# Decoder layer on one core: self attention scores by four row tiles, formed a second time transposed with the maximum subtracted in PSUM

## The chip, the core and the metric

One core of a Trainium2 chip runs the whole layer in one launch. The metric is the device time in microseconds (us); the kernel before took 193.94 us, the median of 3 runs (193.43 to 194.21). All positions in time below count from the first instruction of the profiled execution.

## What is computed

x has 16 sequences of 64 tokens and 128 features; all arithmetic is float32.

```python
x = x + self_attn(layernorm(x))          # 16 heads of 8, rotary embedding, softmax over 64 keys
x = x + cross_attn(layernorm(x), ctx)    # 8 heads of 64, context 16 x 64 x 96
x = x + moe(layernorm(x))                # 2 shared experts + top 2 of 8 experts, SwiGLU, F = 176
# self attention, per sequence b and head h:
attn = softmax(einsum('bhsd,bhtd->bhst', rope(q) * 8**-0.5, rope(k)))
out  = einsum('bhst,bhtd->bhsd', attn, v)
```

## The kernel before

The kernel is one hand ordered program for each engine; each engine works its own list from top to bottom, and semaphores tie the lists together. The chain of TensorE calls is at the end of the tensor block (lines 1185 to 1275), that of ScalarE at 530 to 608, of VectorE at 820 to 916 and of GpSimd at 356 to 398.

**Self attention (units 0 to 15).** Sequences go in four quads of 4 sequences (256 tokens); heads in four groups g of 4 heads. A unit u is quad u // 4, group u % 4. `queries_keys(quad)` projects (L930 to L932, lines of a helper of three float16 matmuls), `rotate(quad)` on VectorE adds bias and rotates (L660, L672). The heads are told apart by masks: `mask_q` writes q four times, once per group with the other rows zero, into qG (L316 on GpSimd; the first quad by `mask_q0`, L679 on VectorE), and `mask_k` writes k four times, once per head of a group, into kM (L323; first quad L452 on ScalarE, second L686 on VectorE). `scores(u)` is then 4 matmuls with all 128 rows (L1006: 64 weight columns, 256 moving columns, two column tiles). Each float32 matmul shows as two records. `shift(u)` on VectorE takes the maximum (L695) and subtracts it on the way out of PSUM (L698), `exponentials(u)` on ScalarE writes ex (L460), `transpose_p(u)` transposes it by 4 matmuls with the identity (L1037), `copy_t(u)` brings that to PT (L469). After four units `attend(quad)` multiplies with the values (L1058) and with ones (L1064, the sums); `divide_ot` divides (L712, L716), `bias_ot` adds the bias (L494), `project_o(hf)` projects half of the tokens (L1076), `add_x2(hf)` adds x. Scores use banks 0 to 2 in turn, so up to three units are under way.

**Cross attention (units 16 to 23)** follows in the same pattern, with `copy_xq`, `shift`, `sums`, `divide` (GpSimd, L346), `transpose_p`, `copy_t`, `cross_attend`, `cross_project`. It needs x2 of the half: `statistics` (L624, L627), `inverse_std` on GpSimd (L308, L310), `normalise` (L638), `transpose_xn` (L959), `copy_xnT` (L430), `rest_xnT` (L647). **The experts** come last (`expert_up`, `spread_w`, `expert_down`; lines 1130 to 1181).

**What else sets the order.** Banks 6 and 7 are handed round by the list MISC: projection i of that list waits until entry i - 2 has been read out, by ScalarE (`copy_v` L445, `copy_cv` L487, `copy_xq` L500, `copy_kx` L414) or VectorE. The expert weights come in 14 chunks through two staging buffers: SP issues the DMA of chunk c when c - 1 chunks are finished (L285, L289), ScalarE casts each chunk to float16 (`chunk_float16`, L425), GpSimd forms the rest (`split_chunk`, L332) and by that frees the buffer. A ScalarE cast waits in its list until the chunk has landed. `MISC` reads, ahead of the experts:

```python
MISC = (["ln1_0", "k_0", "q_0", "k_1", "q_1", "ln1_1", "v_0", "cv_0", "cv_1", "k_2", "q_2", "v_1",
         "k_3", "q_3", "cv_2", "cv_3", "wo_0", "ln2_0", "kx_4"] ...
```

Of the kernel before, what the change touches and what calls it, by code (L numbers as in the profile page):

```python
# [55 lines left out]
         "k_3", "q_3", "cv_2", "cv_3", "wo_0", "ln2_0", "kx_4"]  # L56
# [7 lines left out]
def decoder_layer(nc, x, ctxT, attn_w, attn_b, bias_rows, xw_q, xw_k, xw_v, xw_o, gate_w, w_gate, w_up,  # L64
# [4 lines left out]
    with ctx:  # L69
# [33 lines left out]
        consts_sb = sb("consts_sb", [P, D + HG + 2 + G + E * E + 2 * 32])  # L103
# [12 lines left out]
        OT = t12  # L116
# [46 lines left out]
        sbank = lambda u: bank[u % 3]  # L163
        tbank = lambda u: bank[3 + u % 2]
# [27 lines left out]
        q0_masked = sem("q0_masked")  # L192
        q_masked = sem("q_masked")
        k_masked = sem("k_masked")
        s_full = sem("s_full")
# [55 lines left out]
        CHUNK_AT = [3, 4, 7, 8, 10, 11, 12, 13, 16, 17, 18, 20, 21]  # L251
        assert len(CHUNK_AT) == len(CHUNKS) + 1
# [44 lines left out]
        def _(pool):  # L297
# [15 lines left out]
            def mask_q(quad):  # L313

                pool.wait_ge(q_rotated, quad + 1)
                nc.gpsimd.tensor_tensor(qG[:, :, quad * QT:(quad + 1) * QT],  # L316
                                        qr[:, quad % 2, :].unsqueeze(1).broadcast_to([D, G, QT]),
                                        mask_g.unsqueeze(2).broadcast_to([D, G, QT]), ALU.mult).then_inc(q_masked, 1)

            def mask_k(quad):  # L320

                pool.wait_ge(k_rotated, quad + 1)
                nc.gpsimd.tensor_tensor(  # L323
                    kM[:, 4 * quad:4 * quad + 4],
                    kr[:, quad % 2, :].rearrange("p (b t) -> p b t", t=S).unsqueeze(2).broadcast_to([D, 4, HG, S]),
                    mask_h4.unsqueeze(1).unsqueeze(3).broadcast_to([D, 4, HG, S]), ALU.mult).then_inc(k_masked, 1)
# [15 lines left out]
            def divide(u):  # L342

                pool.wait_ge(r_ready, u - NU1 + 1)
                v = ex[:, u % NE, :].rearrange("p (c t) -> p c t", t=S)
                nc.gpsimd.tensor_tensor(v, v, rs[:, u % NE, :].unsqueeze(2).broadcast_to([P, BLK, S]),  # L346
                                        ALU.mult).then_inc(p_ready, 1)
# [14 lines left out]
            rest([xwq_sb[:, i] for i in range(2)], xwq_raw, 2)  # L362
            nc.gpsimd.memset(VM[:], 0.0).then_inc(zeroed, 1)
            nc.gpsimd.memset(wT[:], 0.0).then_inc(zeroed, 1)
# [4 lines left out]
            nc.gpsimd.memset(PTx[:], 0.0).then_inc(zeroed, 1)  # L369
            mask_q(1)  # L370
            mask_q(2)
            mask_k(2)
            for c in range(3):
                split_chunk(c)
            mask_q(3)
            mask_k(3)
            for c in range(3, 8):
                split_chunk(c)
            inverse_std(2)
            split_chunk(8)  # L380
            x2_bias(0)
            for u in range(NU1, NU):
                divide(u)
                if u == 16:
                    inverse_std(3)
                if u == 17:
                    split_chunk(9)
                    split_chunk(10)
                if u == 19:
                    x2_bias(1)  # L390
                if u == 23:
                    inverse_std(4)
                if u in (20, 21):
                    split_chunk(u - 9)
# [6 lines left out]
        def _(act):  # L401
# [30 lines left out]
            def copy_v(hf):  # L432

                if hf == 0:
                    act.wait_ge(zeroed, 1)
# [19 lines left out]

            def exponentials(u):
                act.wait_ge(s_sub, u + 1)
                if u >= NE:
                    act.wait_ge(t_full, u - NE + 1)
                nc.scalar.activation(ex[:, u % NE, :], sh[:, u % 2, :], ACT.Exp,  # L460
                                     scale=SCALE1 if u < NU1 else SCALE2).then_inc(e_ready, 1)

            def copy_t(u):

                act.wait_ge(t_full, u + 1)
                if u < NU1:
                    if u >= NPT:
                        act.wait_ge(pv_full, (u - NPT) // 4 + 1)
                    nc.scalar.copy(PT[:, u % NPT, :], tbank(u)[:, :]).then_inc(t_copied, 1)  # L469
                else:  # L470
                    if u == NU1:
                        act.wait_ge(zeroed, 3)
                    if u >= NU1 + 2:
                        act.wait_ge(pv_full, 4 + u - 2 - NU1 + 1)
                    src = tbank(u)[:, :].rearrange("p (c s) -> p c s", s=S)
                    for j in range(2):
                        r = slice(j * S, (j + 1) * S)
                        ins = nc.scalar.copy(PTx[r, u % 2, :, j, :], src[r])  # L478
                    ins.then_inc(t_copied, 1)
# [16 lines left out]
            def copy_xq(hf):  # L496
                act.wait_ge(s_full, NU1 if hf else NU1 // 2)
# [42 lines left out]
            for j in range(NU + 4):  # L540
                if j == 16:
                    copy_t(14)
                    copy_t(15)
                if j == 18:
                    copy_kx(7)
                    copy_t(16)
                    copy_xnT(2, 1)
                    copy_cv(4)
                if j == 19:
                    copy_xq(1)  # L550
                    copy_t(17)
                    copy_otx(0)
                if j == 15:
                    copy_kx(4)
                if j == 17:
                    bias_ot(3)
                if j < NU:
                    exponentials(j)
                if j == 0:
                    copy_xnT(1, 1)  # L560
                    copy_v(0)
                if j in (1, 2):
                    copy_cv(j - 1)
                if j in (9, 12):
                    bias_ot(j // 3 - 3)
                if j == 16:
                    bias_ot(2)
                if 2 <= j < NU + 2 and not 16 <= j <= 19:
                    copy_t(j - 2)
                if j == 3:  # L570
                    copy_kx(3)
                if j == 4:
                    copy_v(1)
                if j in (9, 12):
                    copy_cv(j // 3 - 1)
                if j == 14:
                    copy_xnT(2, 0)
                if j == 15:
                    copy_xq(0)
                if j == 16:  # L580
                    copy_kx(5)
                if j == 17:
                    copy_kx(6)
                if NU1 < j - 3 < NU:
                    copy_otx(j - 3 - NU1)
                if j == 25:
# [748 lines left out]
```

## Time and profile before

| | |
|---|---|
| runs, median (lowest to highest) | 193.94 us (193.43 to 194.21) |
| profiled execution, span from first to last instruction | 190.1 us |
| its own device time | not listed beside the runs; the median lies 3.8 us above the span |
| TensorE matmuls busy | 165.1 us, 87% |
| TensorE weight loads busy | 103.2 us, 54% |
| VectorE, ScalarE, GpSimd busy | 134.7, 115.7, 81.8 us |
| mean granted clock of TensorE | 0.986 |

Busy time of TensorE counts overlapping matmuls once, and ends are modelled, so how long a group of matmuls holds the engine is read from the start of one group to the start of the next. The chain that ended last spends 53% of the span on TensorE, 16% on VectorE, 14% on ScalarE, 5% on GpSimd. Lines such as L930 to L932 belong to a helper and carry the projections of all stages.

### The profile page before, as it was taken

How to read it: one execution, taken by the hardware profiler on the slowest of the kernel's cores; microseconds unless marked ns; L12 is line 12 of the kernel's file. 1: busy time of each engine (PE TensorE's matmuls, PEld its weight loads, DVE VectorE, ACT ScalarE, POOL GpSimd, SP SyncE). 2: the span in 40 equal slices, each digit the busy share in tenths (PEclk: the TensorE clock that was granted, in tenths of full speed). 3: DMA queues.
4: the chain of work that ended last, by engine and by line, in shares of the span. 5: the costliest groups of instructions: out<-in, count | busy, mean ns of one | idle time of the engine just before them, and what ended most of it. 6: DMA issues, size and time to landing. Idle time of an engine off the chain costs nothing.

```text
span 190.1 us, 4163 instructions
## 1 busy us (share of the span) xinstructions
PE 165.1 (87%) x1599; PEld 103.2 (54%) x1599; DVE 134.7 (71%) x279; ACT 115.7 (61%) x227; POOL 81.8 (43%) x78
## 2 busy tenths in 40 slices
PE   7576985999999689849999799997998799999992
PEld 2134543665657346635757687653664566666661
DVE  3468998969989627986184554888787987556642
ACT  2148178795788385658779974653649344555450
POOL 1459560847445000763052440074443455544540
PEclk9999999999999999996999999999999999999997
DMA  5980000031221200100000000000000001000001
GB/s 143 304 280 0 0 2 3 0 84 56 59 58 57 78 0 3 59 14 2 10 0 3 2 3 0 0 5 0 0 3 2 0 3 38 17 0 3 2 3 55
DMA packets 6900, 6.43 MB, mean 34 GB/s; under 512 B 736, under 2 KB 5312, under 8 KB 6880
## 3 DMA queue, kind: packets, MB, share of 16 engines
q1 hardware_dynamic: 6480, 5.63, 10.0%
q10 hardware_dynamic: 400, 0.53, 0.9%
q8 instruction: 13, 0.21, 0.5%
q14 instruction: 7, 0.06, 0.1%
HBM read 5.63 MB, written 0.52 MB: 32 GB/s over the span
## 4 chain that ended last, share of the span: by engine, by line
PE 53%; DVE 16%; ACT 14%; issue 7%; POOL 5%; DMA 3%; POOLq 1%; DVEq 0%; ACTq 0%
PE bank L930 6%; PE bank L1006 6%; PE bank L932 6%; PE bank L931 6%; DVE xn_sb L638 4%; PE bank L1175 4%; PE bank L1037 4%; PE bank L1100 4%; ACT Vx L487 3%; PE bank L1110 3%; DMA x_sb<-x_dram 3%; PE bank L1179 2%; POOL rstd L310 2%; PE bank L1159 2%; ACT ex L460 2%
## 5 line engine op out<-in xcount | busy, mean ns | idle before, releaser
L339 POOL TENSOR_TENSOR qG<-qG 128x512 f16<-128x512 f32 (+1 forms) x26 | 30.1, 1157 | 38.4 <-ACT qG L527 38.3
L520 ACT ACTIVATE qG<-bank 128x512 f32<-128x512 f32 (+1 forms) x28 | 16.7, 597 | 24.4 <-PE bank L932 24.4
L798 DVE TENSOR_TENSOR qG<-bank,qG 128x512 f32<-128x512 f32 (+1 forms) x28 | 19.3, 690 | 13.0 <-PE bank L932 11.5
L695 DVE TENSOR_REDUCE mx<-bank 128x8 f32<-128x512 f32 x24 | 16.3, 680 | 6.1 <-PE bank L1022 4.5
L527 ACT CAST qG<-qG 128x512 f16<-128x512 f32 (+1 forms) x28 | 17.1, 612 | 5.5 <-DVE qG L802 3.5
L460 ACT ACTIVATE ex<-sh 128x512 f32<-128x512 f32 x24 | 15.2, 632 | 6.6 <-DVE sh L698 6.5
L1006 PE MATMUL bank<-kM,qG 128*64 128x256 f32 x128 | 16.9, 390 | 1.3 <-DVE qG L679 1.3
L1175 PEld LDWEIGHTS bank<-wd_sb,qG 128*128 128x128 f16 (+1 forms) x224 | 14.7, 98 | 6.2 <-ACT qG L527 0.7
L698 DVE TENSOR_TENSOR sh<-bank,mx 128x512 f32<-128x512 f32 x24 | 16.6, 692 | 1.6 <-ACT ex L460 0.8
L1175 PE MATMUL bank<-wd_sb,qG 128*128 128x128 f16 (+1 forms) x224 | 17.1, 219 | 0.6 <-ACT qG L527 0.6
L802 DVE TENSOR_TENSOR qG<-bank,qG 128x512 f32<-128x512 f32 x22 | 15.2, 692 | 0.7
L1037 PE MATMUL bank<-consts_sb,ex 128*128 128x128 f32 x96 | 14.8, 277 | 0.0
L1037 PEld LDWEIGHTS bank<-consts_sb,ex 128*128 128x128 f32 x96 | 11.1, 141 | 6.3 <-issue 5.3
L332 POOL TENSOR_TENSOR wd_sb<-stage,wd_sb 128x512 f16<-128x512 f32 (+2 forms) x5 | 4.3, 864 | 20.7 <-ACT wd_sb L425 20.7
L487 ACT COPY Vx<-bank 64x256 f32<-64x256 f32 x32 | 11.7, 367 | 2.3 <-PE bank L990 1.9
L346 POOL TENSOR_TENSOR ex<-ex,rs 128x512 f32<-128x512 f32 x8 | 8.4, 1044 | 11.0 <-DVE rs L707 11.0
L469 ACT COPY PT<-bank 128x512 f32<-128x512 f32 x16 | 9.3, 586 | 3.9 <-PE bank L1037 3.8
L950 PE MATMUL bank<-ctxT_sb,xwk_sb 128*128 128x512 f32 x16 | 10.4, 738 | 1.3 <-issue 1.3
L1006 PEld LDWEIGHTS bank<-kM,qG 128*64 128x64 f32 x128 | 8.0, 136 | 6.4 <-issue 2.2
L1100 PE MATMUL bank<-PTx,Vx 128*64 128x128 f32 x128 | 9.6, 296 | 2.0 <-ACT PTx L478 2.0
L414 ACT ACTIVATE kxM<-bank,consts_sb 128x512 f32<-128x512 f32 x16 | 10.0, 684 | 1.7 <-PE bank L950 1.7
L1179 PE MATMUL bank<-wd_sb,qG 128*128 128x128 f16 (+1 forms) x112 | 10.8, 219 | 0.1
(131 smaller groups left out, 380.7 us busy)
## 6 DMA issues: line engine op xcount, KB each, us to landing
stage<-w_gate_dram SPq DMA_DIRECT2D x3, 256.0 KB, 6.6
stage<-w_up_dram SPq DMA_DIRECT2D x3, 256.0 KB, 2.6
stage<-w_down_dram SPq DMA_DIRECT2D x3, 256.0 KB, 2.9
x_sb<-x_dram SPq DMA_DIRECT2D x2, 256.0 KB, 5.7
out_dram<-x_sb SPq DMA_DIRECT2D x2, 256.0 KB, 2.3
ctxT_sb<-ctxT_dram ACTq DMA_DIRECT2D x1, 384.0 KB, 4.7
sel_sb<-selector_dram SPq DMA_DIRECT2D x1, 352.0 KB, 6.4
qG<-attn_w_dram SPq DMA_DIRECT2D x1, 320.0 KB, 5.9
```

The costliest lines, as they stand in the source:

```text
L339: nc.gpsimd.tensor_tensor(hs[0:r, u % 2, 1, :], hh[0:r, u % 2, :], hs[0:r, u % 2, 0, :], ALU.subtract).then_inc(h_lo, 1)
L460: nc.scalar.activation(ex[:, u % NE, :], sh[:, u % 2, :], ACT.Exp, scale=SCALE1 if u < NU1 else SCALE2).then_inc(e_ready, 1)
L487: ins = nc.scalar.copy(Vx[h2 * S:(h2 + 1) * S, 2 * p + b2, :, :], src)
L520: nc.scalar.activation(sg[0:r, u % 2, :], gbank(u)[0:r, :], ACT.Silu).then_inc(sg_ready, 1)
L527: nc.scalar.copy(hs[0:r, u % 2, 0, :], hh[0:r, u % 2, :]).then_inc(h_hi, 1)
L695: link(nc.vector.reduce_max(mx[:, u % 2, :], v, AX.X))
L698: nc.vector.tensor_tensor(sh[:, u % 2, :].rearrange("p (c t) -> p c t", t=S), v, mx[:, u % 2, :].unsqueeze(2).broadcast_to([P, BLK, S]), A ...
L798: nc.vector.tensor_tensor(dst, ubank(u)[0:r, :], sg[0:r, u % 2, :], ALU.mult).then_inc(hu_ready, 1)
L1006: ins = mm(sbank(u)[b2 * S:(b2 + 1) * S, pp * HG * S:(pp + 1) * HG * S], qG[:, g, b * S:(b + 1) * S], kM[:, b].rearrange("p i t -> p (i t) ...
L1037: ins = nc.tensor.transpose(tbank(u)[:, c * P:(c + 1) * P], ex[:, u % NE, c * P:(c + 1) * P], ident)
L1100: ins = mm(o[c * S:(c + 1) * S, j, :, b2, :], Vx[:, 2 * p + b2, hp, :], PTx[:, u % 2, 2 * hp + b2, :, :], start=True, stop=True)
L1175: mm(pvb[:, n * P:(n + 1) * P], hs[0:r, u % 2, 0, n * P:(n + 1) * P], w[s], start=(first and n == 0 and s == 0), stop=False, skip_group_ch ...
```

## The change

The scores of self attention are formed twice per quad. qG, `mask_q`, `mask_q0`, `mask_k1` and the self attention calls of `shift`, `transpose_p` and `copy_t` go. `first_scores(quad)` works on the rotated q itself in four row tiles of 32 rows (one per group of heads) and two column tiles, into banks 0 to 3. `maxima` reduces each bank to 128x8 into ms. `transpose_max` turns the maxima by 4 matmuls into bank 4, `copy_mT` copies them to mT. `shifted_scores` then overwrites banks 0 to 3: one matmul per row tile, with two rows, writes minus the maximum into all 512 columns, and 8 matmuls per row tile (k as weights, 128 columns; q moving, 64 columns) add the scores transposed. `exponentials` reads that from PSUM and writes PT. `NPT` is 8; PTx of cross attention now lies in PT, OT has memory of its own, ms lies in sh and mT in ex.

```diff
+            def first_scores(quad):
+                pe.wait_ge(q_rotated, quad + 1)
+                pe.wait_ge(k_masked, quad + 1)
+                if quad == 0:
+                    pe.wait_ge(kx_free, 1)
+                else:
+                    pe.wait_ge(e_ready, 4 * quad)
+                for pp in range(2):
+                    for b2 in range(2):
+                        b = 4 * quad + 2 * pp + b2
+                        for g in range(G):
+                            r = slice(32 * g, 32 * (g + 1))
+                            t = (2 * pp + b2) * S
+                            ins = mm(qbank(g)[b2 * S:(b2 + 1) * S, pp * HG * S:(pp + 1) * HG * S],
+                                     qr[r, quad % 2, t:t + S], kM[r, b].rearrange("p i t -> p (i t)"),
...
+            def transpose_max(quad):
+                pe.wait_ge(max_ready, 4 * quad + 4)
...
+                for c in range(HG):
+                    ins = nc.tensor.transpose(mbank[:, c * P:(c + 1) * P], ms[:, c, :], ident)
+            def shifted_scores(quad):
+                pe.wait_ge(mT_copied, quad + 1)
+                for g in range(G):
+                    r = slice(32 * g, 32 * g + 2)
+                    mm(qbank(g)[:, :], minus_h[r, :], mT[r, :], start=True, stop=False, skip_group_check=True)
+                for c in range(HG):
+                    pp, a = c // 2, c % 2
+                    for b2 in range(2):
+                        b = 4 * quad + 2 * pp + b2
+                        for g in range(G):
...
+                            ins = mm(qbank(g)[:, (2 * c + b2) * S:(2 * c + b2 + 1) * S],
+                                     kM[r, b, 2 * a:2 * a + 2].rearrange("p i t -> p (i t)"),
+                                     qr[r, quad % 2, t:t + S], start=False, stop=last, skip_group_check=True)
```

The new orders, condensed, each in its engine's list (p counts the cross units from 0; several calls stand on one line):

```
TensorE
    first_scores(0)
    context_keys(3)
    transpose_xn(1, 1)
    values(0)
    transpose_max(0)
    context_values(0)
    shifted_scores(0)
    first_scores(1)
    context_values(1)
    queries_keys(2)
    attend(0)
    transpose_max(1)
    values(1)
    shifted_scores(1)
    context_values(2)
    first_scores(2)
    queries_keys(3)
    attend(1)
    transpose_max(2)
    context_values(3)
    shifted_scores(2)
    project_o(0)
    first_scores(3)
    attend(2)
    context_keys(4)
    transpose_max(3)
    shifted_scores(3)
    transpose_xn(2, 0)
    cross_queries(0)
    context_keys(5)
    attend(3)
    cross_scores(0)
    cross_scores(1)
    context_keys(6)
    project_o(1)
    cross_scores(2)
    cross_scores(3)
    context_keys(7)
    transpose_p(0)
    context_values(4)
    transpose_xn(2, 1)
...
VectorE
    rotate(0)
    normalise(1, x_sb)
    rotate(1)
    for quad in range(4):
        for g in range(G):
            maxima(4 * quad + g)
        if quad == 0: rest_xnT(1), rotate(2)
        if quad == 1: divide_ot(0), rotate(3), the split of gate_sb
        if quad == 2: divide_ot(1), add_x2(0), statistics(2)
        if quad == 3: normalise(2), divide_ot(2), rest_xnT(2)
    divide_ot(3), shift(0), shift(1), sums(0), add_x2(1), statistics(3), sums(1), normalise(3)
...
ScalarE
    copy_kx(3), copy_xnT(1, 1)
    for quad in range(4):
        copy_mT(quad)
        for g in range(G):
            exponentials(4 * quad + g)
        if quad == 0: copy_v(0), copy_cv(0), copy_cv(1), chunk_float16(0)
        if quad == 1: copy_v(1), bias_ot(0), copy_cv(2), chunk_float16(1), chunk_float16(2)
        if quad == 2: bias_ot(1), copy_cv(3), chunk_float16(3), (4), (5)
    copy_kx(4), copy_xnT(2, 0), bias_ot(2), copy_xq(0), copy_kx(5), copy_kx(6), bias_ot(3)
    chunk_float16(6), (7), cross_exponentials(0), chunk_float16(8), cross_exponentials(1), chunk_float16(9)
...
GpSimd
    memset(ms); memset(VM); mask_k(1); memset(wT); xb_sb; mask_k(2); split_chunk(0); mask_k(3)
    split_chunk(1) to split_chunk(5)
    pool.wait_ge(pv_full, 3)
    nc.gpsimd.memset(PT[:, 0:4, :], 0.0)
    inverse_std(2); x2_bias(0); split_chunk(6) to split_chunk(8)
    divide(0); inverse_std(3); divide(1) ...
```

In MISC "cv_2" moves ahead of "k_3" and "kx_4" ahead of "ln2_0".

## Rows read from the trace of the kernel before

**Rows 1.** The page of before: busy time by engine; granted clock of TensorE in 40 slices of 4.75 us.
```profile
PE 165.1 (87%) x1599; PEld 103.2 (54%) x1599; DVE 134.7 (71%) x279; ACT 115.7 (61%) x227; POOL 81.8 (43%) x78
...
PEclk9999999999999999996999999999999999999997
```

**Rows 2.** Windows: length, busy us of PE, PEld, DVE, ACT, POOL (instructions), granted clock, DMA.
```profile
34.00:58.00 24.00, 24.00 (x314) 14.83 (x314) 21.11 (x34) 19.82 (x45) 13.84 (x10) 1.00 0.20 55
...
83.00:86.00 3.00, 1.40 (x12) 1.26 (x14) 2.79 (x6) 0.99 (x3) 0.86 (x1) 0.94 0.08 22
85.00:88.00 3.00, 3.00 (x25) 2.23 (x23) 2.76 (x6) 2.67 (x7) 0.00 (x0) 0.61 0.07 19
...
120.00:190.00 70.00, 62.83 (x551) 38.48 (x548) 49.94 (x91) 35.54 (x61) 31.32 (x28) 0.99 0.03 9
```

**Rows 3.** Timeline of TensorE, 84.6 us: the second half's normalised x2 is transposed.
```profile
84.61 0.63 PE L959 MATMUL bank<-consts_sb,xn_sb 128*128 128x128 f32 x4 [2.40 <-DVE xn_sb L638]
```

**Rows 4.** Timeline of TensorE in self attention: start, length, line, shape, count.
```profile
50.95 1.10 PE L1058 MATMUL bank<-PT,VM 128*32 128x64 f32 x64
51.87 1.05 PE L1064 MATMUL bank<-PT,consts_sb 128*32 128x256 f32 x16
52.84 0.66 PE L1037 MATMUL bank<-consts_sb,ex 128*128 128x128 f32 x4
53.43 1.08 PE L1006 MATMUL bank<-kM,qG 128*64 128x256 f32 x8
54.45 1.12 PE L990 MATMUL bank<-xwv_sb,ctxT_sb 128*128 128x512 f32 x2
55.41 0.60 PE L1037 MATMUL bank<-consts_sb,ex 128*128 128x128 f32 x4
```

**Rows 5.** Groups by line and shape on VectorE and ScalarE.
```profile
L695 DVE TENSOR_REDUCE mx<-bank 128x8 f32<-128x512 f32 x24 | 16.3, 680 | 6.1 <-PE bank L1022 4.5 <-PE bank L1006 1.4
...
L520 ACT ACTIVATE qG<-bank 128x512 f32<-128x512 f32 x26 | 15.5, 597 | 24.2 <-PE bank L932 24.2
...
L712 DVE RECIPROCAL rsum<-bank 128x256 f32<-128x256 f32 x4 | 7.0, 1753 | 0.5 <-PE bank L1064 0.4
```

**Rows 6.** Groups by line and shape, weight loads: busy, mean ns of one | idle before.
```profile
L1006 PEld LDWEIGHTS bank<-kM,qG 128*64 128x64 f32 x128 | 8.0, 136 | 6.4 <-issue 2.2 <-DVE qG L679 1.6
L1110 PEld LDWEIGHTS bank<-xwo_sb,t 128*128 128x128 f32 x64 | 7.7, 191 | 1.7 <-issue 1.5 <-DVE xb_sb L733 0.2
...
L1058 PEld LDWEIGHTS bank<-PT,VM 128*32 128x32 f32 x256 | 3.8, 110 | 1.1 <-issue 0.7 <-ACT PT L469 0.4
```

**Rows 7.** Timeline of ScalarE, 16 us: the key mask of the first quad.
```profile
16.09 1.71 ACT L452 ACTIVATE kM<-qkr,consts_sb 128x256 f32<-128x256 f32 x4 [0.63 <-DVE qkr L672]
```

**Rows 8.** Timeline of all engines, 25 to 32 us: a projection waits for bank copies.
```profile
25.52 1.73 ACT L445 COPY VM<-bank 64x128 f32<-64x128 f32 x8 [1.26 <-PE bank L932]
...
27.93 1.50 ACT L487 COPY Vx<-bank 64x256 f32<-64x256 f32 x4
...
30.52 0.87 DVE L660 SCALAR_TENSOR_TENSOR t<-bank,attn_b_sb,rope_sb 128x256 f32<-128x256 f32 x2
31.43 0.42 DVE L672 TENSOR_TENSOR qkr<-t 128x256 f32<-128x256 f32 x1
...
31.67 0.28 PE L930 MATMUL bank<-xnT,attn_w_sb 128*128 128x256 f16 x1 [1.28 <-ACT Vx L487]
```

**Rows 9.** DMA issues: KB each, median us from issue to landing.
```profile
stage<-w_up_dram SPq DMA_DIRECT2D x3, 256.0 KB, 2.6
stage<-w_down_dram SPq DMA_DIRECT2D x3, 256.0 KB, 2.9
```

**Rows 10.** Groups by line and shape on GpSimd.
```profile
L310 POOL TENSOR_TENSOR rstd<-ve,minus_half 128x4 f32<-128x4 f32 x6 | 6.2, 1039 | 0.5
...
L332 POOL TENSOR_TENSOR wd_sb<-stage,wd_sb 128x512 f16<-128x512 f32 x3 | 3.5, 1155 | 18.8 <-ACT wd_sb L425 18.8
...
L369 POOL MEMSET PTx<- 128x2048 f32 x1 | 1.8, 1796 | 0.0
```

More of the change, by code:

```diff
@@ L454, in mask_k0, with copy_mT @@
                 ins.then_inc(k_masked, 1)
-            def exponentials(u):
[L457 to L479, printed above, removed]
+            def copy_mT(quad):
+                act.wait_ge(mT_full, quad + 1)
+                if quad:
+                    act.wait_ge(shifted_full, 4 * quad)
+                nc.scalar.copy(mT, mbank[:, :]).then_inc(mT_copied, 1)
@@ new lines, in copy_t @@
+            def copy_t(p):
+                act.wait_ge(t_full, p + 1)
+                if p == 0:
+                    act.wait_ge(zeroed, 4)
+                if p >= 2:
+                    act.wait_ge(pv_full, 4 + p - 2 + 1)
+                src = tbank(p)[:, :].rearrange("p (c s) -> p c s", s=S)
+                for j in range(2):
+                    r = slice(j * S, (j + 1) * S)
+                    ins = nc.scalar.copy(PTx[r, p % 2, :, j, :], src[r])
+                ins.then_inc(t_copied, 1)
@@ L539, in _ @@
             copy_kx(2)
[L540 to L560, printed above, removed]
-                    copy_v(0)
[L562 to L572, printed above, removed]
-                    copy_v(1)
[L574 to L586, printed above, removed]
-                    copy_xnT(3, 0)
-                if j == 19:
-                    copy_cv(5)
-                if j == 20:
-                    copy_cv(6)
-                if j == 21:
-                    copy_cv(7)
-                if j == 27:
-                    router_exp(0)
-                if j in CHUNK_AT:
-                    chunk_float16(CHUNK_AT.index(j))
@@ new lines, in _ @@
+            copy_kx(4)
+            copy_xnT(2, 0)
+            bias_ot(2)
+            copy_xq(0)
+            copy_kx(5)
+            copy_kx(6)
+            bias_ot(3)
+            chunk_float16(6)
+            chunk_float16(7)
+            cross_exponentials(0)
+            chunk_float16(8)
+            cross_exponentials(1)
+            chunk_float16(9)
+            copy_kx(7)
+            copy_t(0)
+            copy_xnT(2, 1)
+            copy_cv(4)
+            cross_exponentials(2)
+            chunk_float16(10)
@@ new lines, in _ @@
+            copy_xq(1)
+            copy_t(1)
+            copy_otx(0)
+            cross_exponentials(3)
+            copy_cv(5)
+            for p in range(4, NT + 3):
+                if p < NT:
+                    cross_exponentials(p)
+                if p - 2 < NT:
+                    copy_t(p - 2)
+                copy_otx(p - 3)
+                if p in (4, 5):
+                    copy_cv(p + 2)
+                    chunk_float16(p + 7)
+                if p == NT + 1:
+                    copy_xnT(3, 0)
@@ L1038, in transpose_p @@
                 ins.then_inc(t_full, 1)
             def attend(quad):
[L1043 removed]
+                pe.wait_ge(e_ready, 4 * quad + 4)
                 if quad % 2 == 0:
@@ new lines, in _ @@
+            first_scores(3)
+            attend(2)
+            context_keys(4)
+            transpose_max(3)
+            shifted_scores(3)
+            transpose_xn(2, 0)
+            cross_queries(0)
+            context_keys(5)
+            attend(3)
+            cross_scores(0)
+            cross_scores(1)
+            context_keys(6)
+            project_o(1)
+            cross_scores(2)
+            cross_scores(3)
+            context_keys(7)
+            transpose_p(0)
+            context_values(4)
@@ L1256, in _ @@
+            for p in range(4, NT):
+                transpose_p(p)
+                cross_attend(p - 1)
+                cross_project(p - 2)
             transpose_xn(3, 0)
```

434 lines of the change are left out of this document (205 added, 229 removed).

## The prediction

> **What bounds the kernel now.** I read the page first. TensorE is busy 87% of the span, at the full granted clock but for one slice [rows 1]. The windows say where: from 34 to 58 us, in self attention, TensorE is never idle, while VectorE is busy for 21.1 and ScalarE for 19.8 of the 24 us [rows 2]. This stage is bound by TensorE's list, with two engines close behind, and it is dense because three score banks keep units in different phases. The experts (120 to 190 us) are not touched; what the change does must show in when cross attention can go on. The landmark for that is the transposition of the normalised second half of x2, at 84.61 us, for which TensorE had waited 2.40 us [rows 3]; behind it the two kernels' lists have nearly the same order. So I walk the new lists to that instruction and compare.
>
> **What goes.** Sixteen units of scores at 1.02 us (53.43 to 54.45) and of transposes at 0.59 (52.84 to 53.43) [rows 4]: 25.8 us of TensorE. On VectorE go 16 subtractions and masks, on ScalarE 16 copies, on GpSimd three q masks. None of it is a gain by itself; it must come off the chain.
>
> **What comes, per quad.** First scores: 16 matmuls of 256 columns, 32 records. Before, 8 records in two column tiles took 1.02 us [rows 4]. If the four row tiles run beside each other, 32 records in 8 tiles are again four deep: 1.0 us; if not, 4.1. Four maxima of 0.68 us [rows 5] overlap a little: 2.5 us. The copy of the turned maxima takes 0.6, as L520 does out of PSUM [rows 5]. Four transposes pass 512 columns once, half of what L990 does in 0.96 (54.45 to 55.41), and took 0.59 behind tiled work [rows 4]; I read 0.15 of that as the change of tiling, and count 0.5 for the turn, and 0.15 ahead of each tiled group. Shifted scores: 8 records of 512 columns in four tiles are two deep, as L990's two records: 0.96 us. Then 64 records with 128 weight columns and only 64 moving ones. The attend has 64 records with 32 weight columns in four column tiles: 0.92 us (50.95 to 51.87), 14 ns each [rows 4]. But a load of 32, 64 and 128 columns lasts 110, 136 and 191 ns [rows 6], some 0.84 ns a column, so 128 columns should hold a tile for about 107 ns (an estimate from that slope); 16 deep, that is 1.7 us, 1.9 with gaps. Together 3.0 us. Lower end 1.9, if the loads hide as the attend's do; upper end 8, if loads of different row tiles queue (64 x 0.107 = 6.8 in place of 1.9), and 10.8 if the 512-column matmuls queue too. I take 3.0: the attend's 14 ns lie below the 27 that a 32-column load needs by the slope, so tiles do load beside each other. Four exponentials out of PSUM, 0.60 each [rows 5], take 2.15 in a row.
>
> A rule of the Trainium skill speaks against this part: TensorE: Matmul & The Clock Gate, section LDWEIGHTS, has a 32x128 load take as long as a 128x128 one, since only columns count. The columns' part agrees (110, 136, 191 ns [rows 6]); no row here shows a 32-row load. With the rule the shifted scores take 3.0 us, and if fewer rows did load faster, 1.9, which is some 3 us less over the quads. The same page, section on packing small matmuls, measured 3.07x for four row tiles of 512 columns; by that the four-fold steps take 1.3 us where I have 1.0, and the sum would be about 1 us more.
>
> **The waits.** Banks 0 to 3 hold both passes, so the first scores of a quad wait for all four exponentials of the quad before: quads no longer overlap. Walk, with 0.05 to 0.15 us from engine to engine:
>
> Quad 0. First scores start at 17.85, behind the key mask that ends at 17.80 [rows 7]. VectorE now does normalise and rotate(1) ahead of the maxima, so these run from 22.0 to 24.5. Turned 25.0; context_values(0) to 26.1 (its bank is freed by rest_xnT(1), behind the maxima); shifted scores to 29.1; exponentials to 31.4.
>
> Quad 1. The maxima stand behind rotate(2) on VectorE, rotate(2) needs queries_keys(2), and that needs banks 7 and 6 read out by copy_cv(0) and copy_cv(1), which now stand behind all four exponentials and copy_v(0): 31.4 + 1.73 + 1.5 + 1.5 = 36.15. Before, the same wait ended at 31.67 [rows 8]. Then q's projection 0.7, rotation 0.87 + 0.42 [rows 8], maxima to 40.8, turned and copied 42.0, shifted scores to 45.05, exponentials 47.35.
>
> Quad 2. copy_v(1), bias 0.5 and copy_cv(2) end at 51.1; projection, rotation and the gate's split at 53.5; maxima 56.0; shifted 60.3; exponentials 62.6. The period is some 15.5 us; before, TensorE's own work set it, 4 x 1.6 + 1.9 for the attend (50.95 to 52.84) [rows 4] = 8.3, and the projections in between.
>
> Quad 3. project_o(0) stands ahead of first scores and waits for bias_ot(1), behind the exponentials: first scores end at 65.25. add_x2 and statistics stand ahead of the maxima: 66.4 to 68.9. copy_mT(3) stands behind the cast of chunk 5, whose DMA waits for split_chunk(3) (66.4) and lands 2.6 later [rows 9]: copied 70.3, shifted 73.35, exponentials 75.65.
>
> First half of x2. GpSimd does split_chunk(5) (70.9), the clear of 2048 columns, 1.80 us, and only then inverse_std(2), 1.04 and a little [rows 10]: 74.0. Normalise 75.7; divide_ot(2), 1.75 [rows 5] + 0.43, stands ahead of rest_xnT(2): 78.6. cross_queries(0), context_keys(5), attend(3): 84.3.
>
> Second half. divide_ot(3) to 86.65; bias_ot(3) stands behind copy_kx(6): 88.95; project_o(1) 90.1; sums(0), ahead of add_x2(1), needs an exponential that stands behind chunks 6 and 7: statistics end at 93.35. Chunk 8's DMA can start only after split_chunk(6) (90.8) and lands 2.9 later [rows 9], cast 94.3. GpSimd does split_chunk(8) 1.16, divide(0) 1.04, inverse_std(3) 1.3 [rows 10]: 97.8; normalise, with GpSimd at work beside it, 2.4: 100.3.
>
> **Sum.** 100.3 - 84.6 = 15.7 us later. The granted clock adds to it: before, it read 0.94 around that wait of 2.40 us and 0.61 in the 3 us from 85 [rows 2, 3]. In the new lists TensorE waits like that, for 1 to 3 us at a time, in each quad, so shifted scores or attends will partly run at 1.2 GHz in place of 2.4. Half of an attend and of a shifted score (2.5 us) is lost per quad where it strikes; I put 2 us on it in all, from 0 to 7. 190.1 + 17.7 = 207.8 us of span; the runs' median lies 3.8 above the span: 211.6, and I say 211.
>
> The Trainium skill, TensorE: Matmul & The Clock Gate, section Loop structure matters more than you think, warns that long waits between bursts of matmuls let the clock drop; by that rule each quad would lose its 2.5 us, and the time would be about 216. The 0.61 agrees with it, and the full clock in 34 to 58 us shows the dense case.
>
> **Rivals.** (a) Row tiles do not run beside each other, or their loads queue: the change does not do what it says. Shifted scores take 8 to 10.8 us instead of 3.0, in three quads wholly on the path: 15 to 23 more, and first scores 2 more: 226 to 236. For: no row shows row tiles. Against: column tiles overlap, loads included. (b) Much of the delay is absorbed: shifted scores take 1.9 (3.3 less), the clock stays up (2 less), and the late bias_ot(3) and chunk 8 (2.3 + 3.5) hide: 211.6 - 11.1 = 200.5, 197 to 203. Against: the path to the landmark goes through both. (c) Faster: TensorE stays the bound. 25.8 us go, 4 x (1.0 + 0.6 + 3.0) = 18.4 come: 7.4 less, 186.5. Its place is the wait for banks 7 and 6 ahead of rotate(2) and rotate(3); it decides if those cost nothing and other work fills the quad's own chain, 1.0 + 2.5 + 0.5 + 0.6 + 3.0 + 2.15 and 0.7 of hand-overs = 10.5 us. Against: 10.5 is itself above 8.3, and one set of banks forbids filling it.
>
> **Chances.** My walk 0.73, (a) 0.12, (b) 0.09, (c) 0.04, no change 0.02. A measurement of this kernel can tell 0.5% from none. The walk's own bounds: 2 of clock, 3.3 of loads and 2 of hand-overs down; 5 of clock and 4 of waits up: 204 to 220. The range, 201 to 222, takes in a part of (b) and leaves (a) and (c) out.
>
> **What would show it.** First scores of a quad right behind the last exponential of the quad before; VectorE idle for some 9 us ahead of quad 1's maxima; 14 to 17 us per quad; the first exponential of quad 1 at about 45, of quad 3 at about 73; the landmark at 99 to 104; a clock below 1 in slices between 35 and 65 us; the experts 70 us as before. Wrong if the period is under 10 us, if the shifted scores take over 5, or if the landmark comes before 90.

## The result: 224.8 us, 16% slower, and the profile after

The kernel with the two passes takes 224.83 us, the median of 4 runs (222.39 to 226.20); the kernel before, run beside it, 193.69 us. The ratio is 1.159, with a 95% interval of 1.150 to 1.168. The forecast was 211, from 201 to 222: the sign was right, the size was not. The profiled execution is the slowest of the four (226.2 us, span 224.4), so positions read from it can lie a microsecond or two later than in the median run.

The page of after, to be read against [rows 1]: busy time by engine, and the granted clock in slices of 5.6 us.

```profile
PE 180.4 (80%) x1839; PEld 113.8 (51%) x1839; DVE 125.9 (56%) x255; ACT 108.8 (48%) x215; POOL 78.6 (35%) x77
...
PEclk9999655875875569569955999999999999999997
```

TensorE is busy for 15 us more, though it was to have 7 less to do, and through self attention its clock is never full for long. The windows of after, with the columns of [rows 2], give the amounts:

```profile
17.00:35.00 18.00, 12.54 (x134) 7.93 (x132) 8.65 (x16) 5.91 (x12) 6.67 (x4) 0.70 0.00 1
35.00:55.00 20.00, 16.02 (x216) 10.16 (x216) 8.00 (x12) 7.19 (x22) 3.18 (x2) 0.67 0.06 16
55.00:75.00 20.00, 14.19 (x204) 8.56 (x202) 9.87 (x14) 6.24 (x19) 4.29 (x3) 0.67 0.07 20
75.00:90.00 15.00, 10.70 (x206) 7.22 (x202) 6.56 (x18) 6.93 (x16) 7.09 (x7) 0.73 0.16 45
90.00:105.00 15.00, 12.26 (x132) 6.30 (x132) 5.73 (x7) 6.87 (x14) 0.00 (x0) 0.70 0.00 1
...
155.00:224.00 69.00, 62.09 (x547) 38.27 (x545) 49.30 (x90) 34.83 (x61) 31.30 (x28) 0.99 0.03 9
```

VectorE and ScalarE, once close behind TensorE [rows 2], are busy for 8.00 and 7.19 of 20 us. The experts take their 70 us as before. Nearly all the loss lies ahead of the landmark, which came 33.7 us later, at 118.31 and not 84.61 [rows 3]; the span grew by 34.3. TensorE's timeline in after (L1001 first scores, L1015 turn of the maxima, L1023 minus the maximum, L1032 scores transposed, L1107 project_o, L954 the landmark):

```profile
17.88 1.12 PE L1001 MATMUL bank<-kM,qkr 32*64 32x256 f32 x32 [0.17 <-issue]
...
25.18 1.11 PE L1015 MATMUL bank<-consts_sb,sh 128*128 128x128 f32 x4 [2.94 <-DVE sh L690]
...
27.93 2.09 PE L1023 MATMUL bank<-ex,consts_sb 2*128 2x512 f32 x8
29.80 3.53 PE L1032 MATMUL bank<-qkr,kM 32*128 32x64 f32 x64
35.56 2.01 PE L1001 MATMUL bank<-kM,qkr 32*64 32x256 f32 x32 [2.23 <-ACT PT L467]
...
41.17 0.28 PE L925 MATMUL bank<-xnT,attn_w_sb 128*128 128x256 f16 x1 [0.32 <-ACT Vx L495]
...
47.00 0.66 PE L1015 MATMUL bank<-consts_sb,sh 128*128 128x128 f32 x4 [3.11 <-DVE sh L690]
...
77.96 2.05 PE L1107 MATMUL bank<-wo_sb,OT 128*128 128x128 f32 x8 [2.57 <-issue]
...
86.07 1.14 PE L1023 MATMUL bank<-ex,consts_sb 2*128 2x512 f32 x8 [0.68 <-ACT ex L460]
87.03 1.91 PE L1032 MATMUL bank<-qkr,kM 32*128 32x64 f32 x64
...
118.31 1.09 PE L954 MATMUL bank<-consts_sb,xn_sb 128*128 128x128 f32 x4 [1.30 <-DVE xn_sb L646]
```

The same instructions stand here at both clocks. Quad 3's shifted scores take 0.96 us to 87.03 and 1.9 more; quad 0's take 1.87 to 29.80 and then 3.53. Ahead of quad 0's, TensorE had waited 2.94 us for the maxima. From 25.2 to 36 us the granted clock reads 0.50 throughout. The turned maxima of quads 0 to 3 begin at 25.18, 47.00, 67.24 and 84.79: 21.8, 20.2 and 17.6 us apart, about 20 in the mean. VectorE in after (L668 and L680 rotation, L690 maxima, L842 split of the gate):

```profile
21.30 1.43 DVE L680 TENSOR_TENSOR qkr<-t 128x256 f32<-128x256 f32 x1
22.66 2.47 DVE L690 TENSOR_REDUCE sh<-bank 128x8 f32<-128x512 f32 x4
...
40.96 0.88 DVE L668 SCALAR_TENSOR_TENSOR t<-bank,attn_b_sb,rope_sb 128x256 f32<-128x256 f32 x2 [15.24 <-PE bank L927]
...
59.06 0.88 DVE L668 SCALAR_TENSOR_TENSOR t<-bank,attn_b_sb,rope_sb 128x256 f32<-128x256 f32 x2 [10.00 <-PE bank L927]
...
62.57 1.12 DVE L842 CAST gate_sb<-gate_raw 128x8 f16<-128x8 f32 x1
```

The waits of 15.24 and 10.00 us stand where the forecast had its wait for banks 6 and 7, but the banks are only a part of them. Behind quad 0's exponentials TensorE has first scores and context values to do, at half clock (35.56 to 39.4); the projection of quad 2's k then starts at once, and that of q waits 0.32 us for a bank copy (41.17). New against the forecast are the addition of 1.43 us, 0.42 in [rows 8], and 1.12 us for a cast of 8 columns.

### The profile page after: what moved, and what is told of

It reads as the page before. It is cut to its first block, busy times and chain, and to the rows that moved or that the text cites. A ratio compares the mean times of both kernels' runs of the same rounds, so it can differ in the third digit from the quotient of the medians.

```text
span 224.4 us, 4553 instructions
## 1 busy us (share of the span) xinstructions
PE 180.4 (80%) x1839; PEld 113.8 (51%) x1839; DVE 125.9 (56%) x255; ACT 108.8 (48%) x215; POOL 78.6 (35%) x77
## 4 chain that ended last, share of the span: by engine, by line
PE 54%; ACT 14%; DVE 13%; issue 10%; POOL 5%; DMA 2%; POOLq 1%; DVEq 0%; ACTq 0%
PE bank L925 6%; PE bank L926 5%; PE bank L927 5%; PE bank L1032 5%; PE bank L1205 3%; DVE sh L690 3%; PE bank L1023 3%; PE bank L1130 3%; PE bank L985 3%; PE bank L945 3%; DVE xn_sb L646 3%; PE bank L1140 2%; ACT PT L467 2%; DMA x_sb<-x_dram 2%; PE bank L1001 2%
## 5 line engine op out<-in xcount | busy, mean ns | idle before, releaser
L798 DVE TENSOR_TENSOR qG<-bank,qG 128x512 f32<-128x512 f32 (+1 forms) x28 | 19.3, 690 | 12.9 <-PE bank L927 11.5
L668 DVE SCALAR_TENSOR_TENSOR t<-bank,attn_b_sb,rope_sb 128x256 f32<-128x256 f32 x16 | 7.0, 476 | 26.6 <-PE bank L927 26.6
L467 ACT ACTIVATE PT<-bank 128x512 f32<-128x512 f32 x16 | 8.3, 602 | 21.4 <-PE bank L1032 21.4
L1205 PE MATMUL bank<-wd_sb,qG 128*128 128x128 f16 (+1 forms) x224 | 17.1, 219 | 0.6 <-ACT qG L534 0.6
L322 POOL TENSOR_TENSOR kM<-qkr,consts_sb 128x1024 f32<-128x1024 f32 x3 | 5.7, 1892 | 33.6 <-DVE qkr L680 33.6
L1032 PEld LDWEIGHTS bank<-qkr,kM 32*128 32x128 f32 x256 | 13.1, 293 | 3.5 <-issue 3.5
L985 PE MATMUL bank<-xwv_sb,ctxT_sb 128*128 128x512 f32 x16 | 13.1, 912 | 0.0
L646 DVE TENSOR_SCALAR xn_sb<-x_sb,mv,rstd 128x128 f32<-128x128 f32 x16 | 8.9, 683 | 6.9 <-POOL rstd L315 6.9
L1032 PE MATMUL bank<-qkr,kM 32*128 32x64 f32 x256 | 12.5, 374 | 0.0
L1015 PE MATMUL bank<-consts_sb,sh 128*128 128x128 f32 x16 | 3.5, 357 | 10.9 <-DVE sh L690 10.9
L715 DVE RECIPROCAL rsum<-bank 128x256 f32<-128x256 f32 x4 | 7.0, 1746 | 8.4 <-PE bank L1095 8.4
L1130 PE MATMUL bank<-PT,Vx 128*64 128x128 f32 x128 | 9.6, 296 | 2.0 <-ACT PT L486 2.0
```

Of the source, the lines that this page charges most:

```text
L646: ins = nc.vector.tensor_scalar(xn_sb[:, hf, n, :], src[:, hf * TPH + n, :], mv[:, hf, n, 0:1], rstd[:, hf, n:n + 1], ALU.subtract, ALU.mult)
L798: nc.vector.tensor_tensor(dst, ubank(u)[0:r, :], sg[0:r, u % 2, :], ALU.mult).then_inc(hu_ready, 1)
L985: mm(ps[:, :], ctxT_sb[:, p * P:(p + 1) * P], xwv_sb[:, :], start=True, stop=True).then_inc(full, 1)
L1032: ins = mm(qbank(g)[:, (2 * c + b2) * S:(2 * c + b2 + 1) * S], kM[r, b, 2 * a:2 * a + 2].rearrange("p i t -> p (i t)"), qr[r, quad % 2, t: ...
L1130: ins = mm(o[c * S:(c + 1) * S, j, :, b2, :], Vx[:, 2 * p + b2, hp, :], PTx[:, p % 2, 2 * hp + b2, :, :], start=True, stop=True)
L1205: mm(pvb[:, n * P:(n + 1) * P], hs[0:r, u % 2, 0, n * P:(n + 1) * P], w[s], start=(first and n == 0 and s == 0), stop=False, skip_group_ch ...
```

## The experiments

Theories after this reading. **Clock**: half the speed in self attention makes up what the forecast lacks. **Order**: the lists, not the added work, make the period; the projections of the next quads, and the copies that free banks 6 and 7 for them, sit behind work that doesn't need them. **Contention**: VectorE is held by GpSimd. **Second pass**: the added work itself is what costs. The medians in this part stand beside runs of the kernel before, which lie between 192.1 and 193.7 by chip. Not all kernels ran on one chip, so the difference of two kernels is given by medians and, in brackets, by ratios times 193.5 us.

**e1_fill.** The lists as in after; in the long waits TensorE multiplies something nobody reads.

```diff
+            def fill(n, copied): ...
+                for _ in range(n):
+                    mm(mbank[:, :], sel_sb[:, 0:P], sel_sb[:, 512:1024], start=True, stop=True)
+            fill(12, 0)    # ahead of transpose_max(0); seven more groups of 3 to 18
```

> The changed kernel with idle matmuls put ahead of the waits of TensorE in self attention (into bank 4, 80 of 128x512 float16 in eight places), lists otherwise as they are. Theory clock: 13 us of the 31 lost are work at 1.2 GHz on the path; with the waits filled the granted clock of 17 to 110 us goes from 0.7 to over 0.95 and the time from 224.8 to about 211 to 214. Rival order: the clock is low only where TensorE waits anyway, the path is set by ScalarE's and VectorE's lists: under 3 us gained, 222 or more.

Measured: 214.3 us, ratio 1.111 (1.102 to 1.120), 0.3 us above the clock theory's range. TensorE's timeline in e1_fill, and its windows from 17 to 90 us:

```profile
25.16 0.66 PE L1015 MATMUL bank<-consts_sb,sh 128*128 128x128 f32 x4 [0.35 <-DVE sh L690]
...
27.77 1.91 PE L1032 MATMUL bank<-qkr,kM 32*128 32x64 f32 x64
...
41.99 0.66 PE L1015 MATMUL bank<-consts_sb,sh 128*128 128x128 f32 x4
...
79.78 4.00 PE L1079 MATMUL bank<-sel_sb 128*128 128x512 f16 x9
...
105.95 1.08 PE L954 MATMUL bank<-consts_sb,xn_sb 128*128 128x128 f32 x4 [1.31 <-DVE xn_sb L646]
```
```profile
17.00:35.00 18.00, 16.20 (x194) 8.73 (x192) 8.60 (x18) 10.02 (x27) 6.65 (x4) 1.00 0.00 1
35.00:55.00 20.00, 16.45 (x320) 10.38 (x321) 11.24 (x19) 9.32 (x25) 5.81 (x4) 1.00 0.06 16
55.00:75.00 20.00, 18.49 (x275) 10.55 (x276) 10.58 (x21) 6.48 (x14) 5.95 (x6) 1.00 0.19 50
75.00:90.00 15.00, 12.14 (x155) 6.14 (x153) 5.14 (x8) 7.91 (x14) 2.82 (x4) 0.77 0.02 5
```

Quad 0's maxima are ready at the same 25.2 us; from there the full clock saves 5.0 us by quad 1 (47.00 to 41.99), 8.1 by quad 2, 12.9 by quad 3 (84.79 to 71.89). The clock costs at least 224.8 - 214.3 = 10.5 us (9.3 by the ratios); at least, since behind 75 us it still read 0.77. There the idle matmuls themselves got in the way: nine of them took 4.00 us from 79.78, at half clock, and cross_queries(0) began behind them at 83.62, though its last input had been written by 81.61.

**e2_order.** The work of after, in another order. ScalarE: copy_v, copy_cv and bias_ot(1) go ahead of each quad's exponentials. TensorE: queries_keys(2) and (3) ahead of the next first scores. VectorE: rest_xnT(1) ahead of the maxima.

```diff
 ScalarE, in quad 0
             copy_mT(quad)
+            copy_v(0); copy_cv(0); copy_cv(1)
             exponentials(...)
-            copy_v(0); copy_cv(0); copy_cv(1)
```

> The changed kernel with the copies of values and context values (copy_v, copy_cv, bias_ot(1)) moved on ScalarE ahead of the exponentials of their quad, their matmuls and queries_keys(2) and (3) ahead of first_scores of the next quad, rest_xnT(1) ahead of the maxima. Nothing added or left out. Theory order: the 15 us and 10 us in which VectorE waited for the projections of quads 1 and 2 go, a quad takes 10.5 to 12 us in place of 18 to 21, and since TensorE waits less the clock comes back too: 197 to 204 us. Rival clock alone: TensorE still waits for maxima and exponentials in each quad, the clock stays at half, and less than 10 us are gained: 215 or more.

Measured: 205.08 us, ratio 1.067 (1.055 to 1.078), 1 us above the theory's range and far from the rival's. The turned maxima now begin at 25.95, 38.23, 51.64 and 62.10. With no idle matmul much of the clock is back too: 0.91 in 17 to 35 us, 1.00 in 35 to 55, then 0.80 in 55 to 75. So the order is worth 19.8 us (17.8), a part of which is clock. How the 19.8 divide, and which of the moves on the three engines gave most, was not tested.

**e4_fill_order.** e2 with 25 idle matmuls in the waits that remain.

> The new order of e2_order with idle matmuls in five of its waits (25 in all, 16 of them in the second half of x2's path). If the order alone brings the clock back, within 2 us of e2_order; if in e2_order the clock stays low in self attention, 3 to 8 us less than e2_order.

Measured: 206.56 us, ratio 1.062 (1.048 to 1.077), not to be told from e2. The clock of 17 to 55 us is 1.00 in e4, and quad 3's turned maxima begin at 61.37 and not 62.10: in self attention the clock had 0.7 us more to give.

**e3_mask.** After, with one wait more: mask_k on GpSimd waits until q is rotated too, so that it no longer runs beside the addition.

```diff
                 pool.wait_ge(k_rotated, quad + 1)
+                pool.wait_ge(q_rotated, quad + 1)
```

> The changed kernel with GpSimd's mask_k(quad) waiting for the rotated q as well as the rotated k. Theory contention: the addition that rotates q (1.43 us in place of 0.42 beside mask_k) is back at 0.42 in three quads, two of them on the path, one with the split of the gate weights behind it: 2 to 4 us gained, 221 to 223. Rival: the mask comes as much later as the addition gains, or the addition is slow for another reason: within 1 us of 224.8.

Measured: 215.23 us, ratio 1.114 (1.103 to 1.125), 9.6 us (8.7) less than after, where 2 to 4 were expected. VectorE, GpSimd and TensorE in e3_mask:

```profile
21.68 0.42 DVE L681 TENSOR_TENSOR qkr<-t 128x256 f32<-128x256 f32 x1
```
```profile
22.24 1.89 POOL L323 TENSOR_TENSOR kM<-qkr,consts_sb 128x1024 f32<-128x1024 f32 x1 [3.28 <-DVE qkr L681]
```
```profile
24.55 0.66 PE L1016 MATMUL bank<-consts_sb,sh 128*128 128x128 f32 x4 [1.93 <-DVE sh L691]
...
27.17 1.91 PE L1033 MATMUL bank<-qkr,kM 32*128 32x64 f32 x64
```

The addition is back at 0.42 us, so TensorE waits 1.93 us for the maxima and not 2.94, and the clock stays full through quad 0's shifted scores (1.91 us and not 3.53); it falls later (0.71 in 35 to 55 us and 0.66 in 55 to 75, with waits of 2.1 to 2.6 us). That suggests that most of the 9.6 us is clock, not contention. **e5_fill_mask**, both edits together, separates the two.

> e1_fill (the waits filled, clock held) with e3_mask's wait of mask_k for the rotated q. e3_mask alone gained 9.6 us where 2 to 4 were expected. Theory contention plus clock: the contention itself is worth 1.0 us on the path in three places, and in e3_mask the rest came from the clock, which kept its full level in quad 0 as the first wait was 1 us shorter; with the clock held by filling, the mask is worth only 2 to 4 us: 210 to 212. Rival: the addition is worth 9 us whatever the clock does: 205.

Measured: 212.59 us, ratio 1.099 (1.092 to 1.106): with the clock held, the mask's wait is worth 1.7 us (2.3) against e1, but the two intervals overlap, and the profiled executions differ by 0.3 us only (spans of 211.9 and 212.2, the landmark at 105.59 and 105.95). So it is worth something between nothing and 4 us, and the rival's 9 is ruled out.

**e6_order_mask.** e2 with the mask's wait, and the split of the gate's weights (two operations of 8 columns) moved ahead of quad 0's maxima.

> e2_order with the wait of mask_k for the rotated q, and with the split of the router's weights (2.1 us beside GpSimd's chunk splits, behind rotate(3)) moved ahead of the first maxima. Theory lists: quads of 10.5 to 11 us in place of 12.3, 13.4 and 10.5; 3 to 5 us gained on e2_order's 205: 200 to 202. Rival (the clock or the first half of x2 sets the end): within 1 us of 205.

Measured: 206.58 us, ratio 1.069 (1.062 to 1.076): a miss. VectorE and GpSimd in e6_order_mask show why:

```profile
23.39 1.46 DVE L838 CAST gate_sb<-gate_raw 128x8 f16<-128x8 f32 x1
...
24.89 2.27 DVE L840 TENSOR_TENSOR gate_sb<-gate_raw,gate_sb 128x8 f16<-128x8 f32 x1
```
```profile
23.88 0.95 POOL L366 MEMSET wT<- 128x1024 f16 x1
24.79 2.34 POOL L369 TENSOR_TENSOR xb_sb<-x_sb,rows_sb 128x1024 f32<-128x1024 f32 x1
```

Each small operation ends where the GpSimd operation beside it ends (24.85 and 24.83, 27.16 and 27.13). The maxima came late, TensorE waited 4.09 us for them, and quad 0's shifted scores began at half clock. **e10_order_gate** puts the split behind quad 0's maxima:

```diff
-            gate split
             maxima(0) ... maxima(3)
+            gate split
             rotate(2)
```

> e6_order_mask once more, with the split of the router's weights put where VectorE and GpSimd both wait (behind quad 0's maxima, ahead of rotate(2)) and not ahead of the first maxima, where its two operations of 8 columns took 1.46 and 2.27 us beside GpSimd's clear and add. Theory contention: these 3.7 us and the half clock of quad 0 that followed go: 199 to 202. Rival: the first half of x2 or something behind it sets the end in both e2_order and e6_order_mask, which is why they are equal: 204 or more.

Measured: 199.48 us, ratio 1.041 (1.037 to 1.044), 7.1 (5.5) less than e6 by that one move. Turned maxima at 25.27, 37.86, 48.29 and 58.75: 12.6 us apart, then 10.4 and 10.5. The first is longer in part for the clock, which fell in quad 0 here too, although from 18 us on TensorE had not once waited longer than 0.71 us. TensorE in e10_order_gate:

```profile
22.88 2.28 PE L989 MATMUL bank<-xwv_sb,ctxT_sb 128*128 128x512 f32 x4 [0.71 <-DVE xnT L659]
...
27.56 3.31 PE L1036 MATMUL bank<-qkr,kM 32*128 32x64 f32 x64
```

**e8_single.** e6 with one pass: it leaves out the first scores, the maxima and the subtraction of the maximum; only the transposed scores remain.

```diff
-            first_scores(q), maxima(4q) to (4q + 3), transpose_max(q), copy_mT(q)
-                    mm(qbank(g)[:, :], minus_h[r, :], mT[r, :], start=True, stop=False, ...)
```

> e6_order_mask without first_scores, maxima, transpose_max, copy_mT and the matmuls that subtract: the exponential is taken of the transposed scores as they are, so the subtraction of the maximum is left out. Theory (the quad's own chain is the limit, and half of it is the first pass): 1.0 + 2.5 + 0.5 + 0.75 + 0.96, some 5.5 us, go from each of four quads, less what VectorE's rotations then show: 12 to 20 us less than e6_order_mask, 182 to 189. Rival (waits on other engines set the period): under 8 us less.

Measured: 191.06 us, ratio 0.988 (0.982 to 0.995), above the 182 to 189 expected, as e6 was above its own range. The difference to e6 is 15.5 us (206.58 - 191.06), but that is not the price of the pass alone: e6 also pays for the gate's split ahead of its maxima. In e8 the split lasts as long (1.47 and 2.27 us) and holds up no maxima; VectorE's next operation, at 28.01, still waited 1.15 us for TensorE. Against e10, where the split is off the chain as well, the difference is 8.4 us (10.1), some 2 a quad. So the first pass, its maxima and the subtraction cost 8 to 10 us beside a good place for the split, and 15.5 beside a bad one.

**e7_tail.** e6 with the end of self attention in another order: the load of w_o, attend(3) and project_o(1) ahead of the keys of chunk 5; inverse_std(2) ahead of the clear of PT; add_x2(1), statistics(3) and bias_ot(3) early.

> e6_order_mask with the lists behind self attention re-ordered: inverse_std(2) ahead of the clear of PT and of split_chunk(5), inverse_std(3) ahead of split_chunk(6) to (8), attend(3) and project_o(1) ahead of context_keys(5), bias_ot(3) ahead of copy_kx(5) and (6), add_x2(1) and statistics(3) ahead of the first shifts, chunk casts spread. Theory: the queues behind self attention cost 8 to 12 us of the 31, as the prediction's walk has them: 188 to 194. Rival: the cross units are not ready earlier, and what is gained ahead of the landmark is lost behind it: 197 or more.

Measured: 200.33 us, ratio 1.038 (1.032 to 1.044), the rival's side: 6.2 us gained, not 12 or more. TensorE in e7_tail:

```profile
87.32 0.66 PE L961 MATMUL bank<-consts_sb,xn_sb 128*128 128x128 f32 x4 [0.50 <-ACT kxM L417]
...
92.59 1.12 PE L1075 MATMUL bank<-consts_sb,ex 128*128 128x128 f32 x4 [4.17 <-POOL ex L346]
```

The landmark came early, and the second transposes behind it then waited 4.17 us for GpSimd's division. It stands behind a chunk split now, for which GpSimd had waited 2.74 us (the cast on ScalarE). **e9_tail2** joins e10 with this tail and splits chunks 6 to 8 in the gap before attend(3).

> e10_order_gate with the lists behind self attention as in e7_tail, and besides chunks 6 to 8 cast and split while ScalarE and GpSimd wait for attend(3), and cross units 0 and 1 shifted and exponentiated ahead of normalise(3) and copy_kx(6), (7); in e7_tail TensorE waited 4.17 us for the second unit behind the landmark. Theory: 191 to 195, level with the kernel before. Rival: cross attention cannot use its inputs earlier: 198 or more.

Measured: 190.90 us (12 runs) beside 192.07 for the kernel before (17 runs): ratio 0.9924 (0.9888 to 0.9959), 0.8% faster than before and 8.6 us (9.3) less than e10. One of the 12 runs took 318.83 us, for a reason that no trace shows, and is not in the ratio. The landmark stands at 81.98, where the kernel before had it at 84.61. TensorE in e9_tail2, then its page's clock row:

```profile
81.98 0.66 PE L960 MATMUL bank<-consts_sb,xn_sb 128*128 128x128 f32 x4 [0.50 <-ACT kxM L416]
82.48 1.04 PE L1074 MATMUL bank<-consts_sb,ex 128*128 128x128 f32 x8
85.91 1.09 PE L1136 MATMUL bank<-PT,Vx 128*64 128x128 f32 x16 [2.39 <-ACT PT L489]
```
```profile
PEclk9957996999999789999999999999999999999997
```

**e11_before_tail.** Is it the tail alone? The kernel before, its scores formed once, with the tail of e9 as far as its lists allow.

> The kernel before, its scores formed once, with the tail of its lists put in the order of e9_tail2: the loads of w_o ahead of the keys of chunk 5, attend(3) and project_o(1) ahead of those keys on TensorE, statistics and inverse_std(3) ahead of GpSimd's last division. Theory A, e9's gain over the kernel before comes from the tail lists and the second pass over the scores only costs: the landmark falls from 84.6 us to 77 to 81 and the time is 184 to 190 us. Theory B, the tail of the kernel before was already as short as its order allows, because its attend(3) was not held by the keys: 191 to 194 us, and then e9's two passes cost nothing.

Measured: 199.26 us, ratio 1.036 (1.030 to 1.042): outside both, and slower. TensorE in e11_before_tail:

```profile
69.44 0.63 PE L1032 MATMUL bank<-consts_sb,ex 128*128 128x128 f32 x4 [2.00 <-ACT PT L468]
...
76.13 0.39 PE L925 MATMUL bank<-xnT,xwq_sb 128*128 128x512 f16 x1 [2.02 <-ACT qG L499]
...
79.58 1.97 PE L1017 MATMUL bank<-kxM,qG 128*64 128x128 f32 x32
...
89.55 1.03 PE L1032 MATMUL bank<-consts_sb,ex 128*128 128x128 f32 x4 [4.00 <-POOL ex L346]
...
92.08 1.06 PE L954 MATMUL bank<-consts_sb,xn_sb 128*128 128x128 f32 x4
```

The first cross scores start at 79.58, where the kernel before had them at 70.86; GpSimd's divisions are late in turn, and the landmark is at 92.08 and not 84.61. The tail that suits the two passes hurts the one pass. Whether another tail would make the kernel before quicker stays open.

**e12_tail2_fill.** e9 with eight idle matmuls.

> e9_tail2 with eight groups of idle matmuls more: two where TensorE waits for the maxima of quad 0, six where it waits for attend(3)'s inputs. Theory A, what is left of the clock term in e9 (its mean granted clock was 0.959) still costs one or two us: 188.5 to 190.5 us. Theory B, the waits that remain are on VectorE and GpSimd, and the clock no longer decides: within 0.5 us of e9's 190.9.

Measured: 191.76 us, ratio 0.982 (0.973 to 0.992). Its six runs spread from 187.94 to 193.31; the ratio rests on the three shortest, the medians alone would give 0.997, and the interval overlaps e9's: undecided. The profiled execution's granted clock is 0.969, against 0.959 in e9.

## Why the prediction was right in sign and wrong in size

**Right: the structure.** The long waits ahead of rotate(2) and rotate(3) are there (15.24 and 10.00 us on VectorE; some 9 was said for the first), one set of score banks chains the quads, project_o(0) waits 2.57 us, and the experts are unchanged. The costs at full clock fit: first scores 1.10 us (1.0 said), four maxima 2.47 (2.5), shifted scores 2.8 to 2.9 (3.0), four exponentials 2.06 (2.15), copy of the maxima 0.59 (0.6). Row tiles do run beside each other: 32 records in 1.10 us, where 8 had taken 1.02 [rows 4], which is 3.7 times as much in the same time, so rival (a) falls. The Trainium skill, TensorE: Matmul & The Clock Gate, section Measured speedup vs the span model, gives 3.07 for four row tiles of 512 columns; the 3.7 here is for 256 columns and eight tiles.

The signs that hang on the length of a quad missed: about 20 us a quad where 14 to 17 were said, the first exponential of quad 1 at 53.92 and not 45, the landmark at 118.31 and not 99 to 104.

**Wrong: the clock term.** The step was "I put 2 us on it in all, from 0 to 7". e1 measures 10.5 or more, above even the upper end. The term counted half an attend and half a shifted score, 2.5 us, in a quad where the clock falls, and took it to fall in less than one quad in all. But in after it is down for more than half of each quad (0.67 to 0.73 in the windows), and what of the quad's chain falls into that time doubles: in quad 0 the shifted scores alone lose 2.6 us (5.4 against 2.8), and the next first scores 0.9 (2.01 against 1.12). Over the quads this adds up to the 12.9 us by which e1 is ahead at the turned maxima of quad 3. The evidence was in [rows 2, 3]: one wait of 2.40 us, then 0.61; the walk itself had put such a wait in each quad. The sentence on the Trainium skill's rule gave about 216, nearer than the sum and still too little. Its own terms give more than it says: 2.5 us in each of four quads on top of 209.6 are 219.6.

**Missing: VectorE held by GpSimd.** e1, with the clock nearly held, is 4.7 us above the walk without its clock term (214.3 against 209.6). Its turned maxima lie 1.2, 3.2 and 3.0 us behind the walk's in quads 1 to 3. In its trace the addition of quad 1 takes 1.23 us, where 0.42 was priced, and ahead of quad 2's maxima the gate's split takes 2.2 us, where the walk left 0.4 for it; e3 has the same two operations at 0.17 us each, where GpSimd had begun nothing ahead of them. The rest lies behind 75 us, where e1's clock is below full, and up to 2.0 us of it are e1's own idle matmuls ahead of cross_queries(0). The walk priced the addition at 0.42 [rows 8], beside which GpSimd was idle, and let mask_k run next to it. The trace of before had shown the dearer case: the same line on VectorE, with GpSimd's addition of x and the bias beside it.

```profile
22.97 0.65 DVE L672 TENSOR_TENSOR qkr<-t 128x256 f32<-128x256 f32 x1
```
```profile
20.97 2.36 POOL L367 TENSOR_TENSOR xb_sb<-x_sb,rows_sb 128x1024 f32<-128x1024 f32 x1 [2.10 <-DVE xn_sb L638]
```

The Trainium skill, SBUF — State Buffer, section Who interferes with whom, states that a VectorE operation with two SBUF inputs contends with a GpSimd operation that reads SBUF, and that one in a two-port mode, which a cast can enter, contends with GpSimd so that whichever began second blocks fully. The runs agree: the addition, the cast and the subtraction stretch until about the end of GpSimd's operation, while the maxima, which read PSUM, stay at 0.62 each beside the same operations.

**Adding up.** 13.2 us lie between the walk's 211.6 and 224.8: 8.5 of clock beyond the 2 counted, and 4.7 of contention, late clock and e1's own idle matmuls. Shown by experiment is the 10.5; of the contention e5 shows only that it is under some 4 us, and the split of the rest is read from traces, not tested.

**Rivals.** (b) and (c) did not come about in this order of the lists. But (c)'s point of decision was the quad's own chain, 10.5 us, and with the waits ahead of rotate(2) and (3) shortened (e10, e9) the last two quads take 10.4 and 10.5: the chain is what then bounds a quad, as worked out. That e9 ends 0.8% ahead of before, in spite of the chain, says that the change was not slow by its work alone: about 20 us were order, clock included (e2). It does not say that two passes are as cheap as one: e8 against e10 has them dearer by 8.4 us, and no run has one pass of this form with e9's tail.

## What to carry to other kernels

Before adding a chain with a wait in it, list what else stands behind that wait in every engine's order: moving a few bank copies and projections forward gave back some 20 of 31 us, the clock's part included. Price each wait of TensorE twice, once for itself and once for the half speed of the matmuls that follow it; idle matmuls in the waits show in one run how much of a loss is clock at the least, as long as they hold up nothing themselves. A run that leaves something out is to be compared with the kernel in which nothing else stands in the way (e8 with e10, not with e6). A list tuned for one structure is no measure of another: the tail that gained with two passes cost 7 us with one.

## What the runs showed of the hardware that was not expected

- With one microsecond less of waiting (1.93 us and not 2.94, e3) TensorE's clock stayed at its full 2.4 GHz through quad 0's shifted scores, and the kernel ended 9.6 us (8.7) sooner. But the length of the last wait alone doesn't decide: in e10 the clock fell at the same place with no wait above 0.71 us since 18 us, and in e3 it was down at the next first scores (2.01 us), behind a wait of 2.23. What does decide, these runs don't show. Small edits ahead of a wait can't be priced by their own length.
- Two VectorE operations of 8 columns took 1.46 and 2.27 us, until the GpSimd operation beside them ended, although they touch none of its data; in e3 they took 0.17 us each. The first began beside mask_k and ended only with the clear behind it, an operation that only writes.
- 64 records of 32 rows, 128 weight columns and 64 moving ones take 1.9 us over four row tiles: 29 ns a record.
